# A GNN message kernel written out in full, with columns for 15 of 16 pairs

## The chip, the core and the metric

The kernel runs on one core of a Trainium2 chip. A time is device microseconds (us) of that core for one execution of the program. The core's engines run in parallel, each through its own list of instructions: TensorE (PE in the profile, PEld for its weight loads), VectorE (DVE), ScalarE (ACT), GpSimd (POOL) and SyncE (SP, which here only issues DMAs). They wait for each other on semaphores. Each engine has a sequencer that reads the list, does register work itself and hands tile instructions to the engine; the profile writes the sequencer's share as DVEq, ACTq and so on.

## The reference

One layer of message passing on a graph of 12,500 nodes (64 features) and 212,500 edges that are sorted by destination (32 features each):

```python
msg_in     = concat(nodes[row], nodes[col], edge_features)      # 64 + 64 + 32
messages   = relu(msg_in @ mW1 + mb1) @ mW2 + mb2               # hidden width 128
aggregated = segment_sum(messages, col, num_segments=12500)
out        = layernorm(nodes + relu(concat(nodes, aggregated) @ uW1 + ub1) @ uW2 + ub2)
```

## The kernel before, in words

**Tiling.** Edges are taken in tiles of 128; eight tiles (1024 edges) are a *pair* in the code's words, and there are 208 pairs, 0 to 207, in 52 iterations `it` of four steps `k`. So p = 4 `it` + `k`. Buffers come in four slots, one per `k`. The last pair holds fewer edges (four tiles and 20 edges).

**The source term.** Ahead of the pairs, TensorE makes the table `table_src` = nodes @ mW1[0:64] in HBM, 128 wide. For most tiles the rows `table_src[src]` of the 128 edges are fetched by one indirect DMA, which GpSimd issues (L717), into `gath`. For pairs 0 to 5 rows of x are fetched in place of rows of the table.

**A tile by columns.** In pairs with `k` = 1, 2 or 3 from iteration 3 on, the eighth tile has no gather. The 128 source numbers of that tile are loaded into a row `col_src` (SyncE, L617); ScalarE and VectorE read them into registers (`TENSOR_LOAD`, L460) and copy, one instruction per edge, the column of x that a register points at from the resident `xdeg` into `col_x` (L469, 64 x 1). L467 works out addresses for three copies at a time. TensorE then multiplies `col_x` with mW1 (L843). Each of the four steps builds 48 columns on ScalarE and 48 on VectorE (`COL_PLAN`), so that four steps serve three tiles: per step a batch of 32 and one of 16 on VectorE, and the same on ScalarE.

**One step (p), engine by engine.** VectorE: adds `gath` to the edge term in PSUM for pair p-1 (L1180, which writes `hid` and counts `hsum_made`); one-hot matrix of pair p (L1150); a register load and 32 column copies; the one-hot and in-degree of pair p+1 in `lhs` (L1158, "turned"); the window start of pair p-3 into a register (L1190), two adds of the window's sums into `agg` and `xdeg` (L1192, L1193); a register load and 16 column copies. ScalarE: relu of pair p-1 (L1007), which waits for the VectorE add; two batches of column copies; the copy of the destination window of pair p+2 (L976). TensorE: sums of pair p-2 (L856, L858), pre-activations of pair p+1 (L832, after L1158 of that pair; L843), window p+3 (L765). GpSimd: eight gathers of pair p, or seven where a tile is built by columns; it waits until VectorE has added pair p-4, whose slot it overwrites. SyncE loads windows, edge features, destinations and, three pairs ahead, the indices `idx` (L566).

**Nodes.** From iteration 6 on each iteration also finishes 256 nodes (`node`, stages UPD, Y, SQUARES, SCALE and PUT at the ends of its four steps): TensorE L896 to L907, ScalarE L1043, L1048, L1051, VectorE L1237 and L1241.

**What sets the order.** Nothing but the order of the code: each engine's list is the order in which `step` and `node` are called in `pairs`. TensorE and VectorE have every iteration written out; ScalarE, GpSimd and SyncE have the first four iterations and the last written out and run the others in two hardware loops (`Fori`).

Of the kernel before, what the change touches and what calls it, by code (L numbers as in the profile page):

```python
# [29 lines left out]
P = 128  # L30
# [23 lines left out]
LAG = 6  # L54
# [30 lines left out]
PEELED = 4  # L85
COL_K = (1, 2, 3)
COL_FIRST = 3
COL_TILE = PT - 1
COL_HALF = P // 2
COL_GROUP = 3  # L90
COL_PLAN = (((2, 0, 32), (1, 48, 16)), ((2, 32, 32), (0, 0, 16)), ((0, 16, 32), (0, 48, 16)), ((1, 0, 32), (1, 32, 16)))
COL_BATCHES = (3, 3, 2)
LAST_ROWS = TILES - 1
LAST_COLS = ((2, LAST_ROWS, P), (0, TILES, TAIL))
LAST_DONE = {2: ((ITERS - COL_FIRST - 1) * COL_BATCHES[2] + 2, (ITERS - COL_FIRST - 1) * COL_BATCHES[2] + 2),
             0: ((ITERS - COL_FIRST) * COL_BATCHES[0] + 1, (ITERS - COL_FIRST) * COL_BATCHES[0])}
# [4 lines left out]
assert RAW <= SLOTS * COL_FIRST and COL_FIRST < PEELED <= LAG and LAST_PAIR % SLOTS == COL_K[-1]  # L101
# [5 lines left out]
def gnn_kernel(nc, x, xT, srcT, dst, dstT, edgeT, mW1, mb1, mW2T, mb2, uW1, ub1, uW2, ub2, out):  # L107
# [4 lines left out]
    with ExitStack() as ctx:  # L112
# [16 lines left out]

        idx_all = sb("idx_all", [P, PEELED * SLOTS * PT], I32)  # L130
        idx = sb("idx", [P, SLOTS, PT], I32)
        raw_x = sb("raw_x", [P, RAW - SLOTS, PT, D])
        raw_t = sb("raw_t", [P, PW])
        gath = sb("gath", [P, SLOTS, PW])
        onehot = sb("onehot", [P, SLOTS, PT * WIN])
# [7 lines left out]
        col_src = sb("col_src", [1, len(COL_K), P], I32)  # L143
        col_x = sb("col_x", [D, len(COL_K), P])
# [92 lines left out]
        idx_in = [sem(f"idx_in{i}") for i in range(SLOTS)]  # L237
# [11 lines left out]
        col_src_in = [sem(f"col_src_in{i}") for i in range(len(COL_K))]  # L249
        cols_act = [sem(f"cols_act{i}") for i in range(len(COL_K))]  # L250
        cols_dve = [sem(f"cols_dve{i}") for i in range(len(COL_K))]
# [47 lines left out]
        def let(eng):  # L299


            eng.sem_inc(passed, 1)  # L302
# [56 lines left out]
        def pairs(eng, step, node, tail, peeled=PEELED, looped=True):  # L359


            for it in range(peeled if looped else LAG):
                for k in range(SLOTS):
                    step(it, k)
            if looped:
                with eng.Fori(peeled, LAG) as it:
                    for k in range(SLOTS):
                        step(it, k)

            def both(it, c):  # L370
                for k in range(SLOTS):
                    step(it, k)
                    for stage in STAGES[k]:
                        node(c, stage, NP)

            if looped:
                with eng.Fori(LAG, ITERS - 1) as it:
                    both(it, it - LAG)
            else:
                for it in range(LAG, ITERS - 1):  # L380
                    both(it, it - LAG)

# [5 lines left out]
            both(ITERS - 1, ITERS - 1 - LAG)  # L388
# [28 lines left out]
        def got(it, k, t):  # L417


            first = (RAW + (k - RAW) % SLOTS) // SLOTS  # L420
            if k in COL_K and not (isinstance(it, int) and it < COL_FIRST):
                return (it - COL_FIRST) * (16 * COL_TILE) + (COL_FIRST - first) * (16 * PT) + 16 * t
            return (it - first) * (16 * PT) + 16 * t

        def has_cols(it, k):

            return k in COL_K and not (isinstance(it, int) and (it < COL_FIRST or (it, k) == (ITERS - 1, COL_K[-1])))
# [3 lines left out]
        def cols_for(it, k, i):  # L431


            at = it + 1 if i == 0 or k == SLOTS - 1 else it
            return None if isinstance(at, int) and not COL_FIRST <= at < ITERS - (COL_K[i] == COL_K[-1]) else at

        def cols_done(it, i):

            return (it - COL_FIRST + 1) * COL_BATCHES[i]

        def last_cols_ready(eng, i):


            built = (ITERS - COL_FIRST - (i == 2)) * COL_BATCHES[i]
            eng.wait_ge(cols_act[i], built)
            eng.wait_ge(cols_dve[i], built)
            eng.wait_ge(col_src_in[i], (ITERS - COL_FIRST) * 16)

        def copy_last(eng, copy, i, start, count, done):


            eng.wait_ge(col_src_in[i], (ITERS - COL_FIRST + 1) * 16)
            eng.wait_ge(pe_steps, steps_for_pre((ITERS - 1) * SLOTS + COL_K[i]) if i == 0 else steps_for_pre((ITERS - 2) * SLOTS + COL_K[i]))
            let(eng)
            copy_batch(eng, copy, i, start, count, done)

        def copy_batch(eng, copy, i, start, count, done):

            regs = [eng.alloc_register(f"col{next(col_regs)}") for n in range(count)]
            eng.load(regs, col_src[0:1, i, start:start + count])  # L460
            for n in range(0, count, COL_GROUP):
                of = []
                for reg in regs[n:n + COL_GROUP]:
                    src = eng.snap(reg, donate=True, min_val=0, max_val=N - 1)
                    of.append(xdeg[0:D, bass.ds(src, 1)])
                for col in of:
                    eng.lower_ap(col)  # L467
                for j, col in enumerate(of):
                    ins = copy(col_x[:, i, start + n + j:start + n + j + 1], col)  # L469
            ins.then_inc(done[i], 1)  # L470

        def copy_cols(eng, copy, it, k, batch, offset, done):


            i, start, count = COL_PLAN[k][batch]
            at = cols_for(it, k, i)
            if at is None:
                return
            if start == 0:
                eng.wait_ge(col_src_in[i], (at - COL_FIRST + 1) * 16)  # L480
                if not (isinstance(at, int) and at == COL_FIRST):
                    eng.wait_ge(pe_steps, steps_for_pre((at - 1) * SLOTS + COL_K[i]))
                let(eng)
            copy_batch(eng, copy, i, start + offset, count, done)

        def p_early(p):

            return isinstance(p, int) and p < PEELED * SLOTS

        def src_by_tile(p, k, j, m):  # L490

            ap = idx_all[0:m, p * PT + j:p * PT + j + 1] if p_early(p) else idx[0:m, k, j:j + 1]
# [55 lines left out]
        def _(sp):  # L548
# [13 lines left out]
            def load_idx(p, it, k):  # L562

                if not (isinstance(p, int) and p < (PEELED + 1) * SLOTS):
                    sp.wait_ge(hsum_made, p - SLOTS + 1)
                sp.dma_start(idx[:, k, :], srcT[:, cols(p * PT, PT)]).then_inc(idx_in[k], 16)  # L566
# [19 lines left out]
            for q, m in TABLE:  # L586
# [5 lines left out]
                if q == Q_PAIRS:  # L592
# [5 lines left out]
                    sp.dma_start(idx_all[:, FIRST * PT:], srcT[:, FIRST * PT:PEELED * SLOTS * PT]).then_inc(idx_rest_in, 16)  # L598
# [4 lines left out]
            def step(it, k):  # L603
# [6 lines left out]
                if pair(it, k, -PREP) and not p_early(pair(it, k, -PREP)[0]):  # L610
                    load_idx(*pair(it, k, -PREP))
                if k < len(COL_K) and not (isinstance(it, int) and not COL_FIRST <= it + 1 < ITERS):
                    if not (isinstance(it, int) and it + 1 == COL_FIRST):
# [720 lines left out]
```

## Time and profile before

| | |
|---|---|
| median of 3 runs | 1922.3 us (1922.01 to 1922.93) |
| the profiled execution | 1922.22 us, of which the span of the profile is 1920.4 us |
| VectorE busy | 1540.8 us, 80% of the span, 10793 instructions |
| GpSimd busy | 1431.4 us, 75%, 1527 instructions |
| TensorE busy | 1429.3 us, 74% (weight loads 1334.2 us) |
| ScalarE busy | 1242.0 us, 65%, 10165 instructions |
| mean granted TensorE clock | 0.804 of full speed |
| DMA | 229.86 MB, 120 GB/s |

Busy time counts tile instructions only. Register work of a sequencer (L460, L467, L1190) is not in it, and neither is the time between two gathers on GpSimd; where an engine stands idle behind such work, the profile puts the idle time down to "issue". An engine at 75% or 80% can therefore be the one that never stops.

### The profile page before, as it was taken

How to read it: one execution, taken by the hardware profiler on the slowest of the kernel's cores; microseconds unless marked ns; L12 is line 12 of the kernel's file. 1: busy time of each engine (PE TensorE's matmuls, PEld its weight loads, DVE VectorE, ACT ScalarE, POOL GpSimd, SP SyncE). 2: the span in 40 equal slices, each digit the busy share in tenths (PEclk: the TensorE clock that was granted, in tenths of full speed). 3: DMA queues.
4: the chain of work that ended last, by engine and by line, in shares of the span. 5: the costliest groups of instructions: out<-in, count | busy, mean ns of one | idle time of the engine just before them, and what ended most of it. 6: DMA issues, size and time to landing. Idle time of an engine off the chain costs nothing.

```text
span 1920.4 us, 56413 instructions
## 1 busy us (share of the span) xinstructions
PE 1429.3 (74%) x8716; PEld 1334.2 (69%) x8716; DVE 1540.8 (80%) x10793; ACT 1242.0 (65%) x10165; POOL 1431.4 (75%) x1527
## 2 busy tenths in 40 slices
PE   6776677777678777767768777776867878777877
PEld 6776566777667677666667667766767767766776
DVE  5568888888888888888888888888888888888883
ACT  3246766767766766766666666766666666766663
POOL 7777777777777777777777777777777777777773
PEclk8898888778877878788887887878788776877686
DMA  9664444444444444444444444444444444444441
GB/s 239 163 154 113 123 114 114 123 115 114 123 113 114 124 115 112 120 118 113 115 123 113 112 122 117 114 119 120 112 115 123 113 114 122 115 114 119 118 109 35
DMA packets 169379, 229.86 MB, mean 120 GB/s; under 512 B 98508, under 2 KB 117687, under 8 KB 168701
## 3 DMA queue, kind: packets, MB, share of 16 engines
q1 hardware_dynamic: 112484, 124.14, 23.4%
q0 software_dynamic: 48416, 97.68, 20.6%
q10 hardware_dynamic: 8254, 5.59, 1.2%
q8 instruction: 75, 1.23, 0.3%
q14 instruction: 150, 1.23, 0.2%
HBM read 217.59 MB, written 9.60 MB: 118 GB/s over the span
## 4 chain that ended last, share of the span: by engine, by line
POOL 63%; issue 23%; PE 4%; DVE 3%; DMA 3%; DVEq 1%; ACT 1%; POOLq 1%; SPq 1%; ACTq 0%
POOL gath L717 63%; DVE col_x L469 2%; DMA gath<-table_src,idx 1%; PE ps_sum L856 1%; DVEq L460 1%; DMA table_src<-gath 1%; PE ps_pre L824 1%; PE ps_pre L825 1%; DVE hid L1180 1%; PE ps_pre L790 0%; PE ps_pre L832 0%; POOLq L302 0%; DMA xwin<-in_xT_dram 0%; ACT hid L1000 0%; DMA col_src<-in_srcT_dram 0%
## 5 line engine op out<-in xcount | busy, mean ns | idle before, releaser
L717 POOL DMA_INDIRECT gath<-table_src,idx x1388 | 1309.6, 944 | 423.0 <-issue 420.6
L469 ACT COPY col_x<-xdeg 64x1 f32 x9428 | 912.4, 187 | 237.6 <-issue 219.6
L832 PE MATMUL ps_pre<-rhs,lhs 128*128 128x128 f32 x3226 | 603.0, 363 | 448.3 <-DVE lhs L1158 445.6
L469 DVE COPY col_x<-xdeg 64x1 f32 x9408 | 718.2, 138 | 216.0 <-issue 215.5
L832 PEld LDWEIGHTS ps_pre<-rhs,lhs 128*128 128x128 f32 x3226 | 558.8, 269 | 477.1 <-DVE lhs L1158 473.9
L856 PE MATMUL ps_sum<-onehot,hid 128*128 128x96 f32 x3322 | 473.2, 304 | 13.0 <-ACT rhs L976 11.9
L856 PEld LDWEIGHTS ps_sum<-onehot,hid 128*128 128x128 f32 x3322 | 463.3, 221 | 23.5 <-issue 15.2
L1007 ACT ACTIVATE hid<-hid 128x1024 f32<-128x1024 f32 x202 | 212.5, 1052 | 180.4 <-DVE hid L1180 177.0
L1180 DVE TENSOR_TENSOR hid<-ps_pre,gath 128x1024 f32<-128x1024 f32 x202 | 246.4, 1220 | 87.2 <-DMA gath<-table_src,idx 75.4
L1158 DVE TENSOR_SCALAR_CACHE_REDUCE lhs<-lhs,place 96x1024 f32<-96x1024 int32 x208 | 264.6, 1272 | 32.7 <-PE ps_sum L765 19.8
L1150 DVE TENSOR_TENSOR onehot<-ps_iota,dst_rel 128x768 f32<-128x768 f32 (+1 forms) x209 | 196.9, 943 | 0.1
L1043 ACT ACTIVATE upd<-ps_node,ub1c 128x256 f32<-128x256 f32 x47 | 22.3, 474 | 163.9 <-PE ps_node L897 155.5
L765 PE MATMUL ps_sum<-w_dst,xwin 65*96 65x128 f32 x416 | 106.5, 343 | 8.1 <-DMA xwin<-in_xT_dram 5.9
L717 POOL DMA_INDIRECT gath<-table_src,idx_all x77 | 74.0, 961 | 25.5 <-issue 22.6
L858 PE MATMUL ps_sum<-ident,deg 96*128 96x96 f32 x416 | 89.5, 301 | 0.0
L843 PE MATMUL ps_pre<-w_src,col_x 64*128 64x128 f32 (+1 forms) x296 | 86.9, 380 | 0.0
L765 PEld LDWEIGHTS ps_sum<-w_dst,xwin 65*96 65x96 f32 x416 | 63.5, 193 | 31.0 <-issue 12.4
L858 PEld LDWEIGHTS ps_sum<-ident,deg 96*128 96x128 f32 x416 | 71.8, 215 | 0.2 <-issue 0.2
L843 PEld LDWEIGHTS ps_pre<-w_src,col_x 64*128 64x128 f32 (+1 forms) x296 | 53.8, 227 | 25.0 <-issue 15.3
L976 ACT COPY rhs<-ps_sum 96x128 f32<-96x128 f32 x208 | 52.8, 255 | 15.7 <-PE ps_sum L765 8.6
L1192 DVE TENSOR_TENSOR agg<-agg,ps_sum 128x96 f32 x208 | 51.3, 247 | 10.2 <-PE ps_sum L858 10.2
L1193 DVE TENSOR_TENSOR xdeg<-xdeg,ps_sum 1x96 f32 x208 | 52.5, 253 | 6.4
(109 smaller groups left out, 639.1 us busy)
## 6 DMA issues: line engine op xcount, KB each, us to landing
lhs<-in_dst_dram SPq DMA_DIRECT2D x207, 384.0 KB
lhs<-in_edgeT_dram SPq DMA_DIRECT2D x207, 128.0 KB
gath<-table_src,idx POOLq DMA_INDIRECT x1388
table_src<-gath SPq DMA_DIRECT2D x12, 512.0 KB, 7.0
xwin<-in_xT_dram SPq DMA_DIRECT2D x208, 24.0 KB
idx<-in_srcT_dram SPq DMA_DIRECT2D x192, 4.0 KB
out_dram<-yout ACTq DMA_DIRECT2D x48, 64.0 KB, 1.6
col_src<-in_srcT_dram SPq DMA_DIRECT2D x148, 0.5 KB
```

Of the source, the lines that this page charges most:

```text
L469: ins = copy(col_x[:, i, start + n + j:start + n + j + 1], col)
L717: pool.indirect_dma_start(gath[0:m, k, j * H:(j + 1) * H], None, table_src, src_by_tile(p, k, j, m)).then_inc(gathered[k], 16)
L765: return nc.tensor.matmul(win(p, k), xwin[:, k, :], w_dst[:, :], start=True, stop=True)
L832: mm = nc.tensor.matmul(to[0:m, j * H:(j + 1) * H], lhs[:, k, j * P:j * P + m], rhs[:, k, :], start=True, stop=not by_cols)
L843: mm = nc.tensor.matmul(to[0:m, j * H:(j + 1) * H], col_x[:, i, 0:m], w_src[0:D, :], start=False, stop=True)
L856: nc.tensor.matmul(bank[:, 0:WIN], hid[0:m, k, j * H:(j + 1) * H], hot(k, j, m), start=(j == 0), stop=(m == TAIL or j == PT - 1))
L858: return nc.tensor.matmul(bank[:, P:P + WIN], deg[0:WIN, k:k + 1].broadcast_to([WIN, P]), ident[0:WIN, 0:WIN], start=True, stop=True)
L976: nc.scalar.copy(rhs[0:WIN, k, :], win(p, k)).then_inc(rhs_made, 1)
L1007: nc.scalar.activation(h, h, ACT.Relu).then_inc(hid_made, 1)
L1150: ins = nc.vector.tensor_tensor(to, nums.broadcast_to([m, t, WIN]), at.broadcast_to([m, t, WIN]), ALU.is_equal)
L1158: nc.vector.tensor_scalar(whole, whole.bitcast(I32), place[0:WIN, cols(p, 1)], 0.0, ALU.is_equal, ALU.add, accum_out=deg[0:WIN, k:k + 1]). ...
L1180: nc.vector.tensor_tensor(hid[:, k, at], ps_pre[k % 2][:, at], gath[:, k, at], ALU.add).then_inc(hsum_made, 1)
```

## The change

1. `pairs` has no hardware loop any more: every engine's list is written out for all 52 iterations.
2. `has_cols(p)`: from pair 13 on every pair has a tile of columns but those whose number is divisible by 16 (`COL_SKIP`), 183 pairs in all, the last among them. Before, it was the pairs with `k` not 0.
3. The 128 columns of a tile are split into 68 for ScalarE and 60 for VectorE. In its step p VectorE builds the last 32 columns of pair p+1 ahead of L1158 of before, and 28 of pair p+2 at the end. ScalarE builds 34 of pair p+1 and 34 of pair p+2. "Spread" are ScalarE's register loads: four of 17 registers, placed ahead of and between the copies, the last two for the next step.
4. VectorE reads window starts four at a time, every fourth step (`load_starts`), and works out the address of pair p-3 ahead of the register load for the columns (`place_sums`).
5. Indices are loaded seven pairs ahead into eight buffers (`AHEAD`), with a wait for VectorE's add of pair p-8 instead of p-4.
6. In the twelve pairs without columns the eighth gather goes to a buffer of its own, `gath_x`, and L1180's add is split into 896 and 128 elements there.

```diff
+EARLY = 16
+COL_FROM = 13
+COL_SKIP = 16
 COL_TILE = PT - 1
+COL_ACT = 68
+COL_LOAD = COL_ACT // 4
+COL_DVE = 28
+AHEAD = 2 * SLOTS
 COL_GROUP = 3
-COL_PLAN = (((2, 0, 32), (1, 48, 16)), ...
...
+        def pairs(eng, step, node, tail):
+            for it in range(ITERS - 1):
+                for k in range(SLOTS):
+                    step(it, k)
+                    if it >= LAG:
+                        for stage in STAGES[k]:
+                            node(it - LAG, stage, NP)
...
+        def has_cols(p):
+            return COL_FROM <= p < PAIRS and p % COL_SKIP != 0
...
+        def load_regs(eng, k, start, count):
+            regs = [eng.alloc_register(f"col{next(col_regs)}") for n in range(count)]
+            eng.load(regs, col_src[0:1, k, start:start + count])
+            return regs
...
+            def load_idx(p):
+                if p >= EARLY + AHEAD:
+                    sp.wait_ge(hsum_made, p - AHEAD + 1)
+                sp.dma_start(idx[:, p % AHEAD, :], srcT[:, cols(p * PT, PT)]).then_inc(idx_in[p % AHEAD], 16)
...
             def step(it, k):        # GpSimd
-                for j, m in tiles_of(p):
-                    if j == rows_of(p) or j == COL_TILE and has_cols(it, k):
-                        break
+                for j, m in tiles_of(p)[0:gathers_of(p)]:
+                    to = gath_x[:, :] if p > COL_FROM and j == COL_TILE else gath[0:m, k, j * H:(j + 1) * H]
...
             def step(it, k):        # ScalarE
-                copy_cols(act, nc.scalar.copy, it, k, 0, 0, cols_act)
-                copy_cols(act, nc.scalar.copy, it, k, 1, 0, cols_act)
+                if has_cols(p + 2):
+                    wait_cols(act, p + 2)
+                    first = load_regs(act, to, 0, COL_LOAD)
+                if has_cols(p + 1):
+                    copy_batch(act, nc.scalar.copy, (k + 1) % SLOTS, 2 * COL_LOAD, act_regs.pop(), cols_act)
+                if has_cols(p + 2):
+                    first += load_regs(act, to, COL_LOAD, COL_LOAD)
+                    copy_batch(act, nc.scalar.copy, to, 0, first, cols_act)
+                    act_regs.append(load_regs(act, to, 2 * COL_LOAD, COL_LOAD) + load_regs(act, to, 3 * COL_LOAD, COL_LOAD))
...
             def step(it, k):        # VectorE
-                copy_cols(dve, nc.vector.tensor_copy, it, k, 0, COL_HALF, cols_dve)
+                if p % SLOTS == SLOTS - 1:
+                    load_starts(p - SLOTS + 1)
+                at = place_sums(p - 3) if p >= 3 else None
+                if has_cols(p + 1):
+                    to, start = (k + 1) % SLOTS, COL_ACT + COL_DVE
+                    copy_batch(dve, nc.vector.tensor_copy, to, start, load_regs(dve, to, start, P - start), cols_dve)
...
-                copy_cols(dve, nc.vector.tensor_copy, it, k, 1, COL_HALF, cols_dve)
+                if has_cols(p + 2):
+                    to = (k + 2) % SLOTS
+                    wait_cols(dve, p + 2)
+                    copy_batch(dve, nc.vector.tensor_copy, to, COL_ACT, load_regs(dve, to, COL_ACT, COL_DVE), cols_dve)
```

VectorE, one step in the middle of the program before; the column copies (L469) and their address work (L467) follow each register load and are cut:

```order
L1180 TENSOR_TENSOR hid<-ps_pre,gath 128x1024 [waits gathered2,pe_steps]
L1150 TENSOR_TENSOR onehot<-ps_iota,dst_rel 128x768 [waits pe_steps]
L460 TENSOR_LOAD col_src [waits col_src_in1,pe_steps]
L467 ISA
L469 COPY col_x<-xdeg 64x1 x3
...
L1158 TENSOR_SCALAR lhs,deg<-lhs,place 96x1024 [waits pe_steps,dst_b_in0]
L1190 TENSOR_LOAD start_i [waits added,pe_steps]
L1190 ISA x2
L1192 ISA
L1192 TENSOR_TENSOR agg<-agg,ps_sum 128x96
L1193 ISA
L1193 TENSOR_TENSOR xdeg<-xdeg,ps_sum 1x96
```

The same step after the change (lines of the changed file: L1169 is the add, L1139 the one-hot matrix, L442 the register load, L453 and L455 the copies):

```order
L1169 TENSOR_TENSOR hid<-ps_pre,gath 128x1024 [waits gathered3,pe_steps]
L1139 TENSOR_TENSOR onehot<-ps_iota,dst_rel 128x768 [waits pe_steps]
L1186 ISA
L442 TENSOR_LOAD col_src
L453 ISA
L455 COPY col_x<-xdeg 64x1 x3
...
L1147 TENSOR_SCALAR lhs,deg<-lhs,place 96x1024 [waits pe_steps,dst_b_in1]
L1195 TENSOR_TENSOR agg<-agg,ps_sum 128x96 [waits added,pe_steps]
L1196 TENSOR_TENSOR xdeg<-xdeg,ps_sum 1x96
L442 TENSOR_LOAD col_src [waits col_src_in2,pe_steps]
```

The load of the window start and its address work have moved from between "turned" and the two adds to one entry, L1186, ahead of the first column load. The first cut stands for 32 copies in both; the second register load is of 16 registers before and of 28 after, and the copies behind it are 16 and 28.

ScalarE, one step in the loop before, which ends with the window copy (L976):

```order
L1007 ACTIVATE hid<-hid 128x1024 [waits hsum_made]
L460 TENSOR_LOAD col_src [waits col_src_in1,pe_steps]
...
L460 TENSOR_LOAD col_src
...
L974 REGISTER_ALU
L297 ISA [waits pe_steps]
L976 COPY rhs<-ps_sum 96x128 [waits added]
```

And after, where L986 is the relu and L953 the window copy:

```order
L986 ACTIVATE hid<-hid 128x1024 [waits hsum_made]
L442 TENSOR_LOAD col_src [waits col_src_in1,pe_steps]
...
L442 TENSOR_LOAD col_src
...
L442 TENSOR_LOAD col_src x2
L953 COPY rhs<-ps_sum 96x128 [waits added,pe_steps]
```

The first cut after the change stands for 34 copies of pair p+1, the second for 34 of pair p+2; before, they are 32 and 16. The two loads ahead of the window copy are new.

## Rows read from the trace of the kernel before

**Rows 1.** The page's first part: busy us, share of the span, instructions.
```profile
PE 1429.3 (74%) x8716; PEld 1334.2 (69%) x8716; DVE 1540.8 (80%) x10793; ACT 1242.0 (65%) x10165; POOL 1431.4 (75%) x1527
```

**Rows 2.** Timeline of GpSimd: start us, duration us, instruction, [idle before].
```profile
1000.24 0.94 POOL L717 DMA_INDIRECT gath<-table_src,idx  x1 [0.30 <-issue]
...
1036.47 0.95 POOL L717 DMA_INDIRECT gath<-table_src,idx  x1 [0.30 <-issue]
```

**Rows 3.** All instructions of L717: ns min/median/max, first and last start.
```profile
L717 POOL DMA_INDIRECT gath<-table_src,idx x1388: 940/944/961, 163.9 to 1895.3; - x199
L717 POOL DMA_INDIRECT gath<-table_src,idx_all x77: 940/944/2121, 64.4 to 162.7; - x77
```

**Rows 4.** Groups of VectorE from 300 to 1800 us: busy us, mean ns, idle before.
```profile
L469 DVE COPY col_x<-xdeg 64x1 f32 x7953 | 607.1, 138 | 182.4 <-issue 182.1
...
L1180 DVE TENSOR_TENSOR hid<-ps_pre,gath 128x1024 f32<-128x1024 f32 x166 | 203.0, 1223 | 67.3 <-DMA gath<-table_src,idx 63.9 <-issue 0.9 <-PE ps_sum L765 0.4
```

**Rows 5.** Timeline of VectorE, one step without a wait.
```profile
439.21 1.22 DVE L1180 TENSOR_TENSOR hid<-ps_pre,gath 128x1024 f32<-128x1024 f32 x1 [0.94 <-DMA gath<-table_src,idx]
...
441.55 2.41 DVE L469 COPY col_x<-xdeg 64x1 f32 x32 [0.24 <-issue]
443.90 1.27 DVE L1158 TENSOR_SCALAR_CACHE_REDUCE lhs<-lhs,place 96x1024 f32<-96x1024 int32 x1
...
445.38 0.25 DVE L1193 TENSOR_TENSOR xdeg<-xdeg,ps_sum 1x96 f32 x1
446.19 1.22 DVE L469 COPY col_x<-xdeg 64x1 f32 x16 [0.56 <-issue]
447.44 1.23 DVE L1180 TENSOR_TENSOR hid<-ps_pre,gath 128x1024 f32<-128x1024 f32 x1
```

**Rows 6.** All register loads of L460, ns min/median/max.
```profile
L460 ACTq TENSOR_LOAD <-col_src x393: 1006/1257/1994, 119.6 to 1889.1; - x197
L460 DVEq TENSOR_LOAD <-col_src x392: 1093/1616/2318, 119.6 to 1882.6; - x196
```

**Rows 7.** Chain of waits, 118 to 150 us, VectorE's sequencer after L1158.
```profile
135.59 0.31 DVEq L1190
...
136.48 0.25 DVEq L460
...
137.75 0.15 DVE col_x L469
```

**Rows 8.** Timeline of VectorE: the node instructions; a hole behind a batch.
```profile
601.38 0.17 DVE L1237 RECIPROCAL stat<-stat 128x2 f32<-128x2 f32 x1
...
601.79 1.21 DVE L1180 TENSOR_TENSOR hid<-ps_pre,gath 128x1024 f32<-128x1024 f32 x1
...
606.95 1.27 DVE L1158 TENSOR_SCALAR_CACHE_REDUCE lhs<-lhs,place 96x1024 f32<-96x1024 int32 x1 [0.31 <-issue]
```

**Rows 9.** Timeline of ScalarE, two steps.
```profile
1013.80 3.06 ACT L469 COPY col_x<-xdeg 64x1 f32 x32 [0.83 <-issue]
1017.11 1.58 ACT L469 COPY col_x<-xdeg 64x1 f32 x16 [0.25 <-issue]
...
1019.52 1.06 ACT L1007 ACTIVATE hid<-hid 128x1024 f32<-128x1024 f32 x1 [0.67 <-DVE hid L1180]
1021.64 4.72 ACT L469 COPY col_x<-xdeg 64x1 f32 x48 [1.07 <-issue]
1026.27 0.26 ACT L976 COPY rhs<-ps_sum 96x128 f32<-96x128 f32 x1
```

**Rows 10.** Windows at either clock: busy us (count) PE, PEld, DVE, ACT, POOL; clock.
```profile
1024.20:1033.20 9.00, 8.90 (x38) 8.27 (x38) 7.44 (x57) 7.02 (x61) 6.87 (x8) 0.50 0.50 133
```

**Rows 11.** Who waited for whom, 300 to 1800 us.
```profile
ACT hid L1007 <- DVE hid L1180: 143.0, 110, 2.7
...
POOL gath L717 <- DVE hid L1180: 2.1, 7, 0.3
```

More of the change, by code:

```diff
@@ L386, in end @@
                 node(c, stage, NP if c < CHUNKS else LAST, i)
-            both(ITERS - 1, ITERS - 1 - LAG)
+            for k in range(SLOTS):
+                step(ITERS - 1, k)
+                for stage in STAGES[k]:
+                    node(ITERS - 1 - LAG, stage, NP)
             end(0, UPD)
@@ L429, in gnn_kernel @@
-        col_regs = count_up()
[L431 to L447, printed above, removed]
@@ L459, in copy_batch, with col_before @@
+        def col_before(p):
+            return next((q for q in range(p - SLOTS, COL_FROM - 1, -SLOTS) if has_cols(q)), None)
+        col_regs = count_up()
+        def load_regs(eng, k, start, count):
             regs = [eng.alloc_register(f"col{next(col_regs)}") for n in range(count)]
-            eng.load(regs, col_src[0:1, i, start:start + count])
-            for n in range(0, count, COL_GROUP):
+            eng.load(regs, col_src[0:1, k, start:start + count])
+            return regs
+        def copy_batch(eng, copy, k, start, regs, done):
+            for n in range(0, len(regs), COL_GROUP):
@@ L915, in _ @@
                 pe.wait_ge(rows_out[0], len(TABLE))
-                pairs(pe, step, node, tail, looped=False)
+                pairs(pe, step, node, tail)
             with pe.Else():
@@ L1179, in add_gathered @@
-                at = slice(0, rows_of(p) * H)
-                nc.vector.tensor_tensor(hid[:, k, at], ps_pre[k % 2][:, at], gath[:, k, at], ALU.add).then_inc(hsum_made, 1)
-            ends = {}
-            def add_sums(p, it, k):
+                    dve.wait_ge(last_made, len(LAST_TILES))
+                spare = p > COL_FROM and not has_cols(p)
+                at = slice(0, (COL_TILE if spare else rows_of(p)) * H)
+                ins = nc.vector.tensor_tensor(hid[:, k, at], ps_pre[k % 2][:, at], gath[:, k, at], ALU.add)
@@ new lines, in add_gathered, with load_starts @@
+                if spare:
+                    at = slice(COL_TILE * H, PW)
+                    ins = nc.vector.tensor_tensor(hid[:, k, at], ps_pre[k % 2][:, at], gath_x[:, :], ALU.add)
+                ins.then_inc(hsum_made, 1)
+            starts = {}
+            def load_starts(p):
+                regs = [dve.alloc_register(f"start{p + i}") for i in range(SLOTS)]
+                dve.load(regs, start_i[0:1, p:p + SLOTS])
+                starts.update((p + i, reg) for i, reg in enumerate(regs))
@@ L1252, in _ @@
             with dve.If(fit == 1):
-                pairs(dve, step, node, tail, looped=False)
+                pairs(dve, step, node, tail)
             with dve.Else():
```

207 lines of the change are left out of this document (84 added, 123 removed).

## The prediction, made blind

> **What bounds the kernel now.** I read the engines' totals first. They name no bound: VectorE 80%, GpSimd 75%, TensorE 74%, ScalarE 65% busy [rows 1]. The timeline of GpSimd does. A gather starts every 1.25 us, 0.94 us of it busy and 0.30 us "issue", without a break [rows 2]; from 163.9 to 1895.3 us there are 1387 intervals for 1388 gathers, so 1.2483 us each [rows 3]. Four pairs have 29 gathers, 36.2 us or 9.05 us per pair, and GpSimd waited for VectorE only 2.1 us in 1500 [rows 11]. So GpSimd sets the pace. The last gather starts at 1895.3 us and the span ends at 1920.4, so about 25 us of tail hang on it.
>
> Next I asked how far behind VectorE is, since the change gives it work. Between 300 and 1800 us it made 166 adds, one per pair: 1500 / 166 = 9.04 us. It waited for gathers 63.9 us of that, 0.385 us per pair [rows 4]. What it needs by itself is therefore 8.65 us per pair: its true load is 96%, not 80%. The missing part is its sequencer: 182 us "issue" ahead of column copies [rows 4], 1.1 us per pair, in which the engine waits until source numbers have been read into registers. Its slack of 0.4 us is the number on which the forecast turns.
>
> **GpSimd's part.** By the lists there were 1388 + 77 gathers [rows 3]. After the change pairs 6 to 12 have 8 (56), of pairs 13 to 206 twelve have 8 and 182 have 7 (1370), the last has 3: 1429, or 36 fewer, times 1.2483 = 44.9 us. Sixteen pairs have 113 gathers, so GpSimd could go at 113 x 1.2483 / 16 = 8.82 us per pair. Writing out its list I cost at nothing: the gathers of the part that was written out already (the 77 with idx_all) have the same median of 944 ns, and the "issue" of 0.30 us is the same in the loop [rows 2, 3]. Indices seven pairs ahead remove no wait that I find: nearly all idle time of GpSimd is "issue". Nothing gained, nothing lost.
>
> **VectorE's part.** One step without a wait is 8.23 us [rows 5]: add to first copy 2.34 (439.21 to 441.55); 32 copies 2.35, so 0.0734 each; L1158 to the second batch 2.29 (443.90 to 446.19); first of 16 copies to the next add 1.25. The rows of register loads lie in two clusters, 16 registers near 1.10 us (the minimum is 1.093) and 32 near 2.1 (the median of an even mix is 1.616, so the other cluster is near 2.1) [rows 6]: 0.0625 us per register. What the change does to a step with both batches:
> - L1186 (address of the window) ahead of the first register load: +0.10. The row nearest is the start block behind L1158, 0.89 us from 135.59 to 136.48, of which 0.31 is the load itself [rows 7]; bounds 0 and 0.58.
> - Second half: that block goes, but two adds and the wait for col_src must still be handed out ahead of the load. Bounds of the gain 0 and 0.89; I take 0.57. The load grows from 16 to 28 registers, +0.75. Net +0.18.
> - 12 more copies at 0.0734: +0.88.
> - Four window starts in one load every fourth step: 0.31 for one [rows 7] plus 3 x 0.0625 is 0.5, so +0.12 per step; bounds 0 and 0.31.
> Sum +1.28. None of it has cover: in this stretch the engine already waits for its sequencer, and a column costs 0.0734 + 0.0625 = 0.136 us, 60 of them 8.2 us, before any tile instruction. In two steps of 16 a batch is absent. Without the first, L1158 follows the one-hot after 2.10 instead of 4.79 us (-2.7); without the second the next add comes 1.73 us after L1158 (445.38 + 0.25 - 443.90) instead of 2.47 + 2.13 (-2.9): 5.6 / 16 = -0.35 per pair.
>
> From above: 8.65 + 1.28 - 0.35 = 9.58. From below: 8.23 + 1.28 - 0.35, plus 0.41 / 4 = 0.10 for the node instructions (601.38 to 601.79) and about 0.2 for holes such as the 0.31 us ahead of L1158 at 606.95 [rows 8]: 9.46. I take 9.50, above GpSimd's 8.82: the bound moves to VectorE, and the 36 gathers saved buy nothing.
>
> A rule of the Trainium skill speaks against this. "Advanced Engine Details and Errata", section Sequencer and Instruction Queues, has it that other engine instructions can be read and queued while the sequencer executes a control instruction; read so, register loads would cost VectorE nothing. The trace agrees for ScalarE only in part (see there) and not for VectorE, where 0.24 and 0.56 us of "issue" stand ahead of the two batches [rows 5]. What the rule would make of the time is the first rival.
>
> **ScalarE and TensorE.** ScalarE's step was relu to first copy 2.12 us with a load of 32 registers, 48 copies with a seam 4.63, window copy 0.26: 7.0 us [rows 9]. Its loads take 1.0 for 16 and 1.96 for 32 [rows 6], so 1.07 for 17. After: 1.3 to the first copy (load 1.07 in place of 1.96, and a wait more), 34 copies at 0.093 = 3.2, a seam of about 0.2 [rows 9], 3.2 again, then two loads of 17 that only the queued copies cover: with a seam of 0.25 behind a load of 1.0 us, some 0.8 to 0.9 are covered, so 1.2 stay open; window copy 0.26. Sum 9.4, plus 0.3 for node work, less 1/16 of both batches (0.5): 9.2 us. It stays beside VectorE with 0.3 us to spare, where it had 2. Its longer list may show holes like VectorE's: 0 to 0.2 us per pair, mostly under queued copies. TensorE at half clock (1.2 GHz) is busy 8.90 of 9.0 us [rows 10], so it too is near the new pace while the clock is low; a column product in 15 of 16 pairs adds a little. Both lie beside VectorE's step, and I add nothing.
>
> **The sum.** The profiled execution took 1922.2 us (span 1920.4, 1.8 around it; the median is 1922.3). Columns run over 195 pairs, 13 to 207: 195 x (9.50 - 9.04) = +90. Start and tail are left as they are. 1922.2 + 90 = 2012 us. With the bounds above VectorE's step goes from 9.1 to 9.9: 1934 to 2090. Its own range, where I expect the errors to be partly independent, is 1975 to 2050.
>
> **The rivals.**
> - *GpSimd stays the bound* (the other side). VectorE's register loads disappear behind queued work, as the rule above would have it. Then its step is 2.10 + 2.35 + 1.73 + 28 x 0.0734 (2.06) = 8.24 us plus node work and holes 0.3, less 0.3, below 8.82: 1922.2 - 44.9 = 1877 us. It decides as soon as VectorE's step is under 8.82, 0.7 below my sum. For it: the start load leaves the second half, and ScalarE shows a load nearly hidden. Against it: the 182 us of issue [rows 4], and that VectorE's copies are no queue to hide behind, since each batch begins only when its load is done. Chance 0.11.
> - *Break-even.* All small terms at their low ends: 9.1 us, 1920 to 1945. Chance 0.07.
> - *ScalarE and TensorE bind as well.* ScalarE waits in each fourth step for TensorE's node product, the relu waits for VectorE (143 us in 1500 before, its slack [rows 11]), and with no slack left each wait of one is passed on. At 9.9 us per pair: +168, 2090 us. Chance 0.10.
> - That the change doesn't do what it says I can exclude for the gathers, copies and loads, which are in the lists.
>
> **How the numbers follow.** Forecast 0.72, GpSimd 0.11, break-even 0.07, coupled 0.10. Predicted 2012 us. The range of 8 in 10 takes the forecast's own, most of break-even and the lower part of the coupled case: 1938 to 2065. Faster by over 0.2% (3.8 us, about what a measurement of this kernel can tell from no change) 0.13, within it 0.02, slower 0.85.
>
> **What would show it.** GpSimd: some 0.6 to 0.7 us of waiting per pair for VectorE's add where there was none, about 130 us in all, and 1429 gathers of unchanged 944 ns. VectorE: no wait for gathers, adds 9.5 us apart, first copy 2.4 us after the add, 2.4 to 2.5 us from the one-hot of pair p+1 (L1147 there) to the second batch, loads of 28 near 1.85 us. ScalarE: hardly any wait for the add. If GpSimd's gathers still follow each other at 1.25 us, the forecast is wrong at VectorE's step; if adds are 9.8 us or more apart and VectorE waits for TensorE, the coupled case is right.

## The result: 3383.9 us, 1.76 times the time before

The changed kernel takes 3383.9 us (median of 4 runs, 3379.3 to 3389.9), the kernel before 1922.2 us beside it (4 runs, 1920.7 to 1922.9): ratio 1.761, 95% interval 1.757 to 1.765. The prediction was 2012 us with a range of 1938 to 2065. The sign was right, the size far off: +1462 us instead of +90.

**Totals.** The page's first part of the changed kernel, to be read against [rows 1] (busy us, share of the span, instructions; the profiled execution took 3379.3 us):

```profile
span 3377.5 us, 59461 instructions
PE 1664.3 (49%) x8788; PEld 1569.9 (46%) x8788; DVE 1668.7 (49%) x12378; ACT 1526.0 (45%) x13201; POOL 1396.9 (41%) x1491
```

No engine is busy for half of the span. VectorE has about the busy time that its instructions ask for: 1541 us before, 1669 now, for 1572 more column copies. A copy kept its length on both engines (median 187 ns on ScalarE and 135 ns on VectorE, before and after). Only TensorE is busy for longer than its 72 more matmuls explain, 1664 us instead of 1429: the mean granted clock was 0.656 here and 0.804 before. It hardly matters, since the chain of waits below gives TensorE 2% of the span. The time is in something that isn't counted as busy, and the page counts no register load as busy.

**The register loads.** All instructions of the loading line (L460 before, L442 now; ns min/median/max, first and last start), against [rows 6]:

```profile
L442 ACTq TENSOR_LOAD <-col_src x733: 1238/3651/3762, 125.3 to 3350.2; - x184
L442 DVEq TENSOR_LOAD <-col_src x366: 1847/2038/2115, 125.3 to 3328.2; - x183
```

VectorE's loads are what the prediction gave them: 28 registers 1.85 us, 32 registers 2.1. ScalarE's are not. A load of 17 was to take 1.07 us; the median is 3.65. The chain of waits shows which ones (start us, us, what; ACTq is ScalarE's sequencer). A piece of the chain can be shorter than the instruction: it is the part of it that the chain follows.

```profile
1500.32 1.14 ACTq L442
...
1501.61 3.65 ACTq L442
...
1505.40 0.84 ACT col_x L455 x8
...
1508.10 0.56 ACT col_x L455 x6
1508.65 2.89 issue
1511.54 3.68 ACTq L442
...
1515.31 0.26 ACT rhs L953
...
1515.84 1.36 ACTq L442
...
1519.77 0.83 ACT col_x L455 x9
1520.60 2.60 issue
...
1525.73 0.83 ACT col_x L455 x9
1526.57 2.61 issue
1529.17 3.68 ACTq L442
...
1532.95 0.04 ACT rhs L953
```

Four loads a pair, each of 17 registers from col_src, starting at words 0, 17, 34 and 51. The first, at word 0, takes 1.24 to 1.42 us in the whole trace, the other three never less than 3.63 (549 loads). The second takes 3.65 (1501.61). The third and fourth stand together between the last copy (1508.65) and the window copy (1515.31): 6.66 us in which the engine has nothing queued. In the pair that begins at 1515.84 the second load, issued while copies are queued, still leaves 2.60 us open. The step from 1500.32 has one batch of copies only, since the pair after it has no columns. "issue" in this view is the part of a load that the chain doesn't give by its line.

**Who waits for that.** The engine waits, whole span (engine, line, waited for: us, times, longest us), against [rows 11]:

```profile
PE ps_sum L833 <- ACT rhs L953: 1662.5, 184, 13.0
POOL gath L699 <- DVE hid L1169: 1330.5, 161, 15.7
DVE lhs L1147 <- PE ps_sum L747: 1217.4, 182, 13.4
ACT rhs L953 <- issue: 1125.8, 176, 6.7
ACT col_x L455 <- issue: 576.4, 310, 7.8
```

Read from below: ScalarE's window copy (L953) stands behind its two last loads, 1125.8 us in 176 pairs, 6.4 us each; TensorE's sums wait for that copy; VectorE's L1147 waits for TensorE; GpSimd's gathers wait for VectorE's add. ScalarE itself waits for the others hardly at all: in the whole span 5.4 us for VectorE's add and 47.0 for its window sums. The page's summary of the chain says the same, share of the span by engine:

```profile
ACT 37%; issue 30%; ACTq 29%; PE 2%; DMA 1%; SPq 1%; DVE 0%
```

One engine's sequencer holds three engines, and no busy share shows it.

**VectorE and GpSimd.** Timeline of VectorE, against [rows 5] (start us, us, instruction, [idle before]):

```profile
1523.81 1.27 DVE L1147 TENSOR_SCALAR_CACHE_REDUCE lhs<-lhs,place 96x1024 f32<-96x1024 int32 x1 [0.67 <-PE ps_sum L747]
...
1526.18 2.10 DVE L455 COPY col_x<-xdeg 64x1 f32 x28 [0.64 <-issue]
1528.32 1.22 DVE L1169 TENSOR_TENSOR hid<-ps_pre,gath 128x1024 f32<-128x1024 f32 x1
...
1530.71 0.87 DVE L455 COPY col_x<-xdeg 64x1 f32 x11 [0.30 <-issue]
1531.79 1.68 DVE L455 COPY col_x<-xdeg 64x1 f32 x21 [0.21 <-issue]
1541.17 1.27 DVE L1147 TENSOR_SCALAR_CACHE_REDUCE lhs<-lhs,place 96x1024 f32<-96x1024 int32 x1 [7.71 <-PE ps_sum L747]
```

And all gathers, against [rows 3]; then the window 400 to 3200 us (length, busy us (count) of PE, PEld, DVE, ACT, POOL; clock, DMA share, GB/s):

```profile
L699 POOL DMA_INDIRECT gath<-table_src,idx x1340: 938/944/961, 162.5 to 3303.2; - x192
L699 POOL DMA_INDIRECT gath<-table_src,idx_all x77: 938/944/2119, 64.4 to 161.3; - x77
...
400.00:3200.00 2800.00, 1359.29 (x6945) 1281.74 (x6945) 1376.99 (x10592) 1285.98 (x11371) 1130.45 (x1199) 0.65 0.24 64
```

VectorE's own parts came out as worked out; then it waits 7.71 us for TensorE. In the 2800 us of the window it made 169 adds: 16.57 us per pair, where the forecast had 9.50. The gathers keep their 944 ns.

### The profile page after: what moved, and what is told of

It is laid out like the page before. It is cut to its first block, busy times and chain, and to the rows that moved or that the text cites. A ratio compares the mean times of both kernels' runs of the same rounds, so it can differ in the third digit from the quotient of the medians.

```text
span 3377.5 us, 59461 instructions
## 1 busy us (share of the span) xinstructions
PE 1664.3 (49%) x8788; PEld 1569.9 (46%) x8788; DVE 1668.7 (49%) x12378; ACT 1526.0 (45%) x13201; POOL 1396.9 (41%) x1491
## 4 chain that ended last, share of the span: by engine, by line
ACT 37%; issue 30%; ACTq 29%; PE 2%; DMA 1%; SPq 1%; DVE 0%
ACT col_x L455 34%; ACTq L442 28%; ACTq L453 1%; ACT rhs L953 1%; ACT sq L1037 1%; ACT upd L1032 1%; PE ps_sum L833 1%; DMA table_src<-gath 0%; ACT hid L986 0%; PE ps_pre L806 0%; PE ps_pre L807 0%; PE ps_pre L772 0%; DMA col_src<-in_srcT_dram 0%; PE ps_pre L813 0%; DMA xwin<-in_xT_dram 0%
## 5 line engine op out<-in xcount | busy, mean ns | idle before, releaser
L699 POOL DMA_INDIRECT gath<-table_src,idx x1340 | 1263.9, 943 | 1863.0 <-DVE hid L1169 1329.2
L833 PE MATMUL ps_sum<-onehot,hid 128*128 128x96 f32 x3322 | 725.1, 408 | 1679.9 <-ACT rhs L953 1662.5
L833 PEld LDWEIGHTS ps_sum<-onehot,hid 128*128 128x128 f32 x3322 | 684.5, 314 | 1720.1 <-issue 1718.3
L455 ACT COPY col_x<-xdeg 64x1 f32 x12464 | 1193.7, 187 | 579.9 <-issue 576.4
L455 DVE COPY col_x<-xdeg 64x1 f32 x10980 | 835.3, 138 | 221.6 <-issue 221.2
L1147 DVE TENSOR_SCALAR_CACHE_REDUCE lhs<-lhs,place 96x1024 f32<-96x1024 int32 x208 | 264.7, 1273 | 1239.4 <-PE ps_sum L747 1217.4
L813 PE MATMUL ps_pre<-rhs,lhs 128*128 128x128 f32 x3226 | 597.8, 363 | 3.0 <-ACTq L981 2.6
L953 ACT COPY rhs<-ps_sum 96x128 f32<-96x128 f32 x208 | 54.0, 261 | 1180.7 <-issue 1125.8
L813 PEld LDWEIGHTS ps_pre<-rhs,lhs 128*128 128x128 f32 x3226 | 585.1, 280 | 3.6 <-issue 2.9
L1169 DVE TENSOR_TENSOR hid<-ps_pre,gath 128x1024 f32<-128x1024 f32 x202 | 244.6, 1211 | 14.6 <-ACTq L981 5.8
L986 ACT ACTIVATE hid<-hid 128x1024 f32<-128x1024 f32 x202 | 211.8, 1048 | 12.1 <-DVE hid L1169 5.4
L1139 DVE TENSOR_TENSOR onehot<-ps_iota,dst_rel 128x768 f32<-128x768 f32 (+1 forms) x209 | 196.9, 942 | 0.1
L835 PE MATMUL ps_sum<-ident,deg 96*128 96x96 f32 x416 | 125.6, 403 | 0.0
L835 PEld LDWEIGHTS ps_sum<-ident,deg 96*128 96x128 f32 x416 | 107.4, 316 | 0.1
L747 PE MATMUL ps_sum<-w_dst,xwin 65*96 65x128 f32 x416 | 95.0, 310 | 6.7 <-DMA xwin<-in_xT_dram 3.8
L747 PEld LDWEIGHTS ps_sum<-w_dst,xwin 65*96 65x96 f32 x416 | 52.1, 163 | 29.9 <-DMA xwin<-in_xT_dram 4.6
```

What stands on the lines that cost most here:

```text
L455: ins = copy(col_x[:, k, start + n + j:start + n + j + 1], col)
L699: pool.indirect_dma_start(to, None, table_src, src_by_tile(p, k, j, m)).then_inc(gathered[k], 16)
L747: return nc.tensor.matmul(win(p, k), xwin[:, k, :], w_dst[:, :], start=True, stop=True)
L813: mm = nc.tensor.matmul(to[0:m, j * H:(j + 1) * H], lhs[:, k, j * P:j * P + m], rhs[:, k, :], start=True, stop=not by_cols)
L833: nc.tensor.matmul(bank[:, 0:WIN], hid[0:m, k, j * H:(j + 1) * H], hot(k, j, m), start=(j == 0), stop=(m == TAIL or j == PT - 1))
L835: return nc.tensor.matmul(bank[:, P:P + WIN], deg[0:WIN, k:k + 1].broadcast_to([WIN, P]), ident[0:WIN, 0:WIN], start=True, stop=True)
```

## The experiments

Four theories. START: a register load whose first word is not a multiple of four (16 bytes) is slow, about 0.21 us per register instead of 0.06. LIST: ScalarE's written-out list makes its loads slow. COUNT: a number of registers that is no multiple of four does. SUPPLY: what comes from memory arrives late, so that it matters how far ahead the indices are loaded; one expectation calls the opposite HIDDEN. COUPLED, in one expectation, is the prediction's rival by which ScalarE and TensorE bind as well. COUNT was weak from the start: the loads of 17 at word 0 took only 1.24 to 1.42 us above.

In all comparisons below the kernel before took 3033 to 3070 us, not 1922; so kernels are compared only with the kernel before of the same comparison, by the ratio. The expectations that give a time for a kernel before of 1922 us, those of e1 to e4 above all, could not be tested in their microseconds. The slower condition is taken up under e5.

**e1, the kernel after with aligned loads.** The same 68 columns in four loads that start on multiples of four words.

```
-        COL_LOAD = COL_ACT // 4                  # loads (0,17) (17,17) (34,17) (51,17)
+        COL_LOADS = ((0, 16), (16, 20), (36, 16), (52, 16))
```

> The changed kernel, but ScalarE's four register loads are of 16, 20, 16 and 16 registers (starts at words 0, 16, 36 and 52 of col_src, each a multiple of four words) instead of four of 17 (starts 0, 17, 34, 51). The 68 copies, the order and everything else stay. Theory START: a register load that starts off a 16-byte boundary pays about 0.2 us per register (3.65 us for 17 where the aligned one of 17 takes 1.25). Then ScalarE's loads fall to about 1.0 and 1.25 us, and the time to the 2012 us of the prediction (range 1960 to 2050), VectorE's adds 9.5 us apart. Rival LIST: ScalarE's loads are slow because its list is written out; then they stay near 3.6 us and the time near 3380. Rival COUNT: a number of registers that is not a multiple of four makes a load slow (this run can't tell it from START, the shifted one can).

3016.3 us, ratio 0.994 (0.991 to 0.996). The loads of e1:

```profile
L442 ACTq TENSOR_LOAD <-col_src x733: 1002/1023/1266, 229.4 to 2975.3; - x184
L442 DVEq TENSOR_LOAD <-col_src x366: 1846/2006/2155, 244.9 to 2970.8; - x183
```

Same written-out list, same number of loads and registers, and all take 1.0 us (16 registers) or 1.25 (20). LIST is wrong. This run alone doesn't part START from COUNT, since 17 went away together with the odd starts; e3 and e9 do.

**e2, the kernel before with its lists written out.**

```
-                pairs(act, step, node, tail)
+                pairs(act, step, node, tail, looped=False)     # and so for SP and GpSimd
```

> The kernel before with all engines' lists written out (no hardware loops), columns, loads and gathers as before. START and COUNT: no difference, 1922 us within 0.5%, ScalarE's loads 1.0 and 1.96 us. LIST: ScalarE's loads become slow (16 registers well above 1.0 us) and the time rises by hundreds of us.

3002.7 us, ratio 0.990 (0.984 to 0.995): written out, the kernel before gains one per cent under these conditions, where START expected no difference within half a per cent. The loads are as in the loop:

```profile
L460 ACTq TENSOR_LOAD <-col_src x393: 1012/1260/2220, 207.9 to 2973.4; - x197
L460 DVEq TENSOR_LOAD <-col_src x392: 1093/1653/2245, 223.8 to 2967.3; - x196
```

**e3, the kernel before with its loads shifted.** Counts stay 16 and 32; the rows of col_src begin 1, 2 or 4 words later, by slot.

```
+        col_at = (1, 2, 4)
-            eng.load(regs, col_src[0:1, i, start:start + count])
+            eng.load(regs, col_src[0:1, i, col_at[i] + start:col_at[i] + start + count])
```

> The kernel before with loops, but the rows of source numbers in SBUF begin one word (slot 0), two words (slot 1) and four words (slot 2) past a 16-byte boundary; loads of 32 and 16 registers on both engines as before. START: loads from slots 0 and 1 take about 0.2 us per register (3.4 us for 16, 6.8 for 32) on ScalarE, and on VectorE as well if its sequencer works the same way; slot 2 keeps 1.0/1.96 and 1.1/2.1. Two thirds of 48 registers per step at 0.15 us more is +4.8 us per pair, some 2850 us. If eight bytes suffice, slot 1 is fast and the time is near 2350. COUNT and LIST: all loads as before, 1922 us.

One run, 3366.7 us (before 3034.3). This settles START against COUNT:

```profile
L461 ACTq TENSOR_LOAD <-col_src x393: 1934/3457/6844, 211.1 to 3331.5; - x197
L461 DVEq TENSOR_LOAD <-col_src x392: 2103/3614/7186, 214.8 to 3325.4; - x196
```

The counts are multiples of four, and the loads are slow. On either engine half of the loads of 32 (the 98 from slot 2, 4 words off) stay at 1.9 to 2.3 us, the other 98 (slots 0 and 1, 1 and 2 words off) take 6.8 to 7.2; loads of 16, which all fell to slots 0 and 1, take 3.4 to 3.7, but for one of 4.3. So a start 4 or 8 bytes off is slow and one 16 bytes off is not, on ScalarE and VectorE alike. The time rose less than expected, by 332 us instead of some 930. That part of the loads lay under waits that the slower conditions had already made is my reading; no run here shows it.

**e5, the kernel before, unchanged: what is different here.**

> The kernel before, unchanged, for a trace beside the other runs. In the last comparison it took 3034 us where it had taken 1922. If that was the place or moment of those runs, it is 1922 us here, or, where it is 3034 again, its trace shows what differs: theory SUPPLY, everything that comes from memory outside the core (instructions, indices, windows) arrives late, so that engines stand at issue and at DMAs; register loads keep 1.0/1.96 and 1.1/2.1 us.

3076.6 us. Its waits and a piece of ScalarE's timeline:

```profile
ACT col_x L469 <- issue: 1405.4, 1701, 2.0
...
POOL gath L717 <- DMA idx<-in_srcT_dram: 1037.9, 134, 11.7
```

```profile
1500.36 0.19 ACT L469 COPY col_x<-xdeg 64x1 f32 x1 [0.53 <-issue]
1501.07 0.19 ACT L469 COPY col_x<-xdeg 64x1 f32 x1 [0.52 <-issue]
1501.80 0.19 ACT L469 COPY col_x<-xdeg 64x1 f32 x1 [0.54 <-issue]
```

Column copies that were 0.09 us apart stand 0.72 apart in stretches, with "issue" between them, on VectorE too, and GpSimd waits 1037.9 us for its indices, of which the first trace has nothing. Register loads and gathers kept their lengths.

Slow transfers are not what these traces show. The two large queues in the page of the first trace, then in e5's (packets, MB, share of 16 engines' span):

```profile
q1 hardware_dynamic: 112484, 124.14, 23.4%
q0 software_dynamic: 48416, 97.68, 20.6%
```

```profile
q1 hardware_dynamic: 112484, 124.14, 14.7%
q0 software_dynamic: 48416, 97.68, 12.5%
```

The packets are the same, and their shares of 1920.4 and 3074.9 us come to 449 and 396 us before, 452 and 384 in e5: a packet takes no longer, the kernel only asks for them more slowly. The wait for indices is in part a late request as well. At 1505.44 VectorE's add ends 5.38 us of "issue"; SyncE, which waits for that add, issues the index load at 1506.83, and GpSimd, idle for 5.53 us, goes on at 1509.32. Only the last 2.5 us are the load. So the engines stand at "issue". The same kernel in both cases, so the code isn't the cause; what is stays open. It means that the prices of single instructions carry over between the two conditions, and the pace of the whole does not.

**e6, e7 and e13, aligned again,** each beside its own runs of the kernel before.

> e1_aligned once more, beside e5. If the kernel before is at 1922 us here, START gives 2012 us (1960 to 2050), with VectorE's adds 9.5 us apart, and LIST 3380. If it is at 3034 again, the ratio is 0.994 as in e1.

> e1_aligned a third time, since in both comparisons so far the kernel before took over 3000 us, with column copies that start 0.7 us apart in stretches where register loads keep their lengths. Where the kernel before is at 1922 us: START gives 2012 us (1960 to 2050), VectorE's adds 9.5 us apart, ScalarE's loads at 1.0 and 1.25 us; LIST gives 3380.

> The kernel with ScalarE's four loads on multiples of four words (16, 20, 16, 16 registers), nothing else changed against the kernel after. If the kernel before takes 1922 us beside it, START and the prediction's other steps expect VectorE's adds 9.4 to 9.6 us apart and 2000 to 2030 us; COUPLED expects adds 9.8 us or more apart with VectorE waiting for TensorE, 2060 us or more; if GpSimd still set the pace it would be near 1877. If the kernel before takes about 3050 us again, all expect the ratio 0.994 of the three comparisons so far, and nothing new is told of the 9.5 us.

Ratios 0.995 (0.992 to 0.998), 0.995 (0.992 to 0.998) and 0.995 (0.993 to 0.998); the kernel before took 3070, 3038 and 3033 us. Four comparisons (with e1) say the same: with aligned loads the change gains half a per cent where the kernel before takes about 3040 us. What it does where that takes 1922 us was not seen.

**e8, the kernel after, unchanged.**

> The changed kernel, unchanged, beside the others under the conditions in which the kernel before takes about 3034 us and e1_aligned 3016. START: its three misaligned loads of 17 registers cost 3 x 2.4 us on ScalarE in 183 pairs, 1318 us; if ScalarE sets the pace here too, the time is near 3016 + 1318 = 4330 us, less what the slower stretches of the other engines cover: 3700 to 4350. LIST: the loads of e1 were fast in a list that is written out as this one is, so LIST has fallen already.

4067.1 us, ratio 1.330 (1.325 to 1.335), inside the expected 3700 to 4350 us. Against e1 (0.994) the edit of the four loads (their starts, and with them 16, 20, 16, 16 registers for four times 17) is worth 0.336 of the kernel before, about 1030 us, and takes the whole loss away. From three slow loads a pair I would have it 3 x 2.4 x 183 = 1318 us. I take the missing fifth to be covered by waits that e1 has anyway; that isn't shown.

**e9, one slow load of four.**

```
+        COL_LOADS = ((0, 16), (16, 18), (34, 18), (52, 16))    # 34 is off
```

> e1_aligned with ScalarE's four loads as 16, 18, 18 and 16 registers, starting at words 0, 16, 34 and 52: one of the four, of 18 registers, starts off a 16-byte boundary (34 words). START: that load takes 0.21 x 18 = 3.8 us instead of about 1.0, the one of 18 from word 16 about 1.4 (16 registers and two by ones). +3 us per pair in ScalarE's sequencer, 183 pairs, 550 us: 3400 to 3600 us if ScalarE sets the pace, 3016 if it does not.

3137.5 us, ratio 1.022 (1.017 to 1.027), 0.028 above e1: about 85 us, below the 3400 to 3600 us expected if ScalarE set the pace and above the 3016 if it didn't. The loads, all of them and then two single ones, that of 18 at word 34 and that of 18 at word 16 (the trace is of the longest of the five executions, 3241.4 us):

```profile
L442 ACTq TENSOR_LOAD <-col_src x733: 1003/1247/4007, 231.3 to 3202.1; - x184
L442 ACTq TENSOR_LOAD <-col_src x1: 3906/3906/3906, 1503.8 to 1503.8; - x1
L442 ACTq TENSOR_LOAD <-col_src x1: 1457/1457/1457, 1515.8 to 1515.8; - x1
```

This is the plainest case against COUNT: on the same engine, in the same trace, 18 registers take 1.46 us from word 16 and 3.9 from word 34. The four loads of a pair take 7.4 us together instead of e1's 4.3, and 183 x 3.1 would be 570 us, so most of it goes where ScalarE had time. Three slow loads cost 0.336, one 0.028. I read that as the first going into slack and the others onto the path; that the one here is the third of the four, and which of e8's three cost most, was not varied.

**e10, indices only as many pairs ahead as before.** e1 with

```
-        AHEAD = 2 * SLOTS
+        AHEAD = SLOTS
```

> e1_aligned with indices loaded three pairs ahead into four buffers, as the kernel before does, instead of seven ahead into eight. Theory HIDDEN (the prediction's): the distance costs nothing, 3016 us within 1%. Rival SUPPLY: GpSimd waited 1038 us for indices in e5, so the distance matters where memory is late, and the time rises by over 2%, to 3080 us or more.

3084.6 us, ratio 1.008 (1.005 to 1.011), 0.014 above e1: more than HIDDEN's one per cent and less than SUPPLY's two. The waits of GpSimd, first e10, then e1:

```profile
POOL gath L699 <- DMA idx<-in_srcT_dram: 973.9, 161, 13.8
```

```profile
POOL gath L699 <- DVE hid L1169: 940.0, 168, 38.4
```

Under these conditions the early indices remove a wait of GpSimd for them; nearly all of it comes back as a wait for VectorE, whose late add also held up the requests for indices (see e5), and 1.4% is left. Where there was no such wait [rows 2, 11] nothing here contradicts a price of nothing.

**e4, e12, e11 and e14, fewer pairs with columns.** The aligned kernel with columns in 13 of 16 pairs (e4, e12) and in 12 of 16 (e11, e14).

```
+        COL_NONE = (0, 4, 8, 12)                 # (0, 6, 11) for 13 of 16
-            return COL_FROM <= p < PAIRS and p % COL_SKIP != 0
+            return COL_FROM <= p < PAIRS and p % COL_SKIP not in COL_NONE
```

> e1_aligned with a tile of columns in 13 of 16 pairs instead of 15. GpSimd then has 115 gathers in 16 pairs, 8.97 us per pair at 1.2483 us each; VectorE by the prediction's terms 9.50 - 2 x 0.35 = 8.80 us. START: GpSimd sets the pace again, 1922 - 195 x 0.08 = 1906 us (1895 to 1925), the only version here expected below the kernel before. LIST: above 3000 us.

> e4 once more: 0.963 of the kernel before under the conditions of e1 to e10; 1906 us, 0.992 of it, where that takes 1922 us.

> e1_aligned with a tile of columns in 12 of 16 pairs, the share that the kernel before has, so that lists, early indices and the 68 to 60 split are what is left of the change. By the prediction's terms GpSimd makes 9.05 us per pair again and VectorE 9.50 - 3 x 0.35 = 8.45: 1922 us where the kernel before takes 1922. Where it takes 3000 to 3070, engines other than GpSimd set the pace, fewer columns help them, and the time is below e4's 0.963 of before, near 0.95; if GpSimd sets it, above 0.97.

> The same with tiles of columns in 12 of 16 pairs. If the kernel before takes 1922 us: GpSimd has 16 x 8 - 12 = 116 gathers in 16 pairs, 116 x 1.2483 / 16 = 9.05 us per pair, VectorE's step 9.5 less 3/16 of both batches' 5.6 (1.05), 8.45: GpSimd sets the pace, 1910 to 1935 us, as before. If it takes about 3050 us again: ratio 0.952.

13 of 16: 2926.9 and 2925.6 us, ratios 0.963 (0.958 to 0.968) and 0.963 (0.957 to 0.969). 12 of 16: 2889.2 and 2900.3, ratios 0.952 (0.946 to 0.958) and 0.956 (0.951 to 0.961). These are faster than both kernels, and e11 is the fastest that was run. More gathers (1465 at 12 of 16, 36 more than after) and fewer copies gain time, so under these conditions GpSimd doesn't set the pace. What does is less clear. In e11 the chain gives VectorE and its sequencer 39% of the span, ScalarE and its sequencer 7%, TensorE 12% and "issue" 35%, and TensorE's L814 waits 668 us for something that the profile doesn't name (766 us at L813 in e1). The column work of VectorE is a part of it, and that is the direction of the prediction's argument on VectorE, under other conditions than the ones it was made for. These versions also show what the change is worth without its extra columns: at 12 of 16 pairs the gathers are 1465 as in the kernel before, and the rest of the change, with aligned loads, gains 4.4 to 4.8%. Written-out lists alone gave 1.0% (e2), early indices 1.4% (e10).

## Why the prediction was wrong

**The step that failed** is in the part on ScalarE: "Its loads take 1.0 for 16 and 1.96 for 32, so 1.07 for 17." All 393 loads behind that line began on a multiple of 16 words. I interpolated over the count and did not ask what else the change altered: `COL_ACT // 4` is 17, and three of four loads begin at words 17, 34 and 51. They take 3.65 us, and the chain of waits runs through them: ScalarE needs 16.57 us per pair instead of 9.2 and sets the pace. Two halves of the error can be told apart. At word 0 a load of 17 takes 1.25 (the minimum of 1238 ns above), so the odd register costs 0.24 instead of 0.06; that is small. The start costs 3.65 - 1.25 = 2.4 us, three times per pair.

With the measured loads the prediction's own sum for ScalarE comes out right. First load +0.18; second load open for 2.6 us instead of 0.2, +2.4; last two open for 6.4 (1125.8 us in 176 pairs) instead of 1.2, +5.2; together 7.8, less a sixteenth for the pairs without columns, 7.3. 9.2 + 7.3 = 16.5 us per pair; measured 16.57. And 195 x (16.5 - 9.04) = 1455 us, on top of 1922.2 that is 3377 for the profiled execution, which took 3379.3. The 9.2 under this was measured in no run, so agreement as close as this is partly luck, but there is no room for a second large cause. The experiment says the same under the slower conditions: the edit of the loads takes the ratio from 1.330 (e8) to 0.994 (e1), and e3 and e9 show that it is the starts and not the counts.

**Point by point.**
- "The bound moves to VectorE" at 9.50 us per pair: not what happened. ScalarE is the bound, and VectorE waited 1217 us for TensorE behind it. Its parts were right: add to first copy 2.39 (1528.32 to 1530.71; 2.44 forecast), L1147 to the second batch 2.37 (1523.81 to 1526.18; 2.47), second batch to the add 2.14 (2.13). Whether they add up to 9.50 when nothing else holds it was not seen in any run. One small term was too high: four window starts in one load take 0.35 us (L1180), not 0.5.
- GpSimd: "1429 gathers of unchanged 944 ns": the lists have 1429, the trace shows 1340 + 77 + 12 = 1429, median 944. Written out its list costs nothing, as said. It waited for VectorE's add 1330 us, not 130.
- "ScalarE hardly waits for the add": right, and for the wrong reason.
- ScalarE "stays beside VectorE with 0.3 us to spare": I had a step of 9.2 us built on five loads and seams, none of them yet seen in this form, and gave it a chance of only 0.10 to bind. The slack was the place to put the uncertainty.
- The rival "ScalarE and TensorE bind as well" had part of the chain (VectorE waits for TensorE, that for ScalarE) and its sign came true, adds more than 9.8 us apart. Its mechanism did not: it had ScalarE wait for VectorE and TensorE and pass that on, and ScalarE waited for them next to nothing (5.4 and 47.0 us for VectorE). Its price of 9.9 us per pair was wrong by the same term as the forecast.
- "GpSimd stays the bound" and break-even: wrong. Reading the sequencer as the place of the cost was right; the rival by which loads vanish behind queued work is refuted on ScalarE: behind queued copies 3.65 us loads stayed open for 2.6 to 2.7, so that some 0.9 to 1.05 us are covered, near the 0.8 to 0.9 that the prediction took from [rows 9].
- The range, 1938 to 2065, was made of the bounds of VectorE's terms and of the lower part of the coupled case. ScalarE's loads of 17 had no bound from above at all. The nearest rows had one condition in common that the new loads didn't share, and that is where a bound "however far" was due.

**What stays open.** Whether the aligned version takes 2012 us where the kernel before takes 1922; why it took about 3040 in all later comparisons; how the slow load works inside (only its price by register is shown); and how much of the slow loads a pair could hide, and in which places.

## What to carry to other kernels

When a size changes, list the start address of each access too, and not only its count: a price read from rows holds for what those rows have in common, here starts on multiples of 16 words. Split a list of numbers that is loaded into registers at multiples of four words, even if the parts become unequal: 16, 20, 16, 16 in place of four times 17 saved a quarter of the time (e8 against e1, ratios 1.330 and 0.994, where the kernel before takes some 3040 us). And look at the sequencer's rows by themselves: a load is counted as busy by no engine, and what stands behind it in program order (here the window copy) passes its length on to the engines that wait for it.

## What the runs showed of the hardware that I had not expected

- A register load from SBUF that begins off a 16-byte boundary. ScalarE: 17 registers 3.65 us instead of 1.25, 16 registers 3.46 instead of 1.01, 32 registers up to 6.84 instead of 1.96, each about 0.21 us per register against 0.06; in e9 18 registers 3.9 instead of 1.46. VectorE: 16 registers 3.61 instead of 1.10, 32 up to 7.19 instead of 2.10, 0.225 per register. 4 and 8 bytes off are slow (e3), and so are the starts at words 17, 34 and 51 of the changed kernel, 4, 8 and 12 bytes off; 16 bytes off is not slow, and neither are VectorE's starts at 272 and 384 bytes.
- Aligned, 16 registers take 1.0 us on ScalarE, 17 take 1.25, 18 take 1.46 (e9) and 20 again 1.25. On VectorE one register takes 0.31 (L1190 before) and four in one load 0.35 (L1180 after). So four aligned words cost about as much as one word, some 0.23 us, and each register left over about as much as one of a load that begins off the boundary; that is worked out from these rows, and no run was made for it.
- The same kernel at 1922 and at 3033 to 3077 us, with unchanged lengths of gathers and register loads, and unchanged time for the same DMA packets, but column copies 0.72 us apart in stretches, with "issue" between them. The cause is open.
